# The output bias of an attention block, added by VectorE ahead of the product or by a matmul behind it

## What is computed

```python
A = jnp.sum(_cos_sim(K) * V, axis=-2)
Y = A[:, None, :] * Q
Y = Y @ W_out + b_out
return Y + X              # X is the row-normalised input here
# around it:
x = x + _layernorm(attn(_layernorm(x, axis=-1), ...), axis=-1)
x = x + _layernorm(ffn(_layernorm(x, axis=-1), ...), axis=-1)
```

## Time and profile before

| | |
|---|---|
| time, median of 3 runs (lowest, highest) | 973.98 us (970.87, 974.26) |
| the profiled execution's own time | 972.4 us |
| its span, first to last instruction | 970.6 us |
| PE busy, matmuls | 890.0 us (92%), 4558 |
| DVE busy | 639.8 us (66%) |
| ACT busy | 435.9 us (45%) |
| POOL busy | 387.7 us (40%) |
| mean granted TensorE clock | 0.974 of full speed |

### The profile page before, as it was taken

One profiled execution on the slowest core, in us unless ns is written; L12 is line 12 of the kernel. 1 busy time (PEld: TensorE's weight loads), 2 busy tenths in 40 slices (PEclk: granted clock), 3 DMA queues, 4 the chain that ended last, 5 costly groups with the idle time before them and its releaser, 6 DMA issues.

```text
span 970.6 us, 14785 instructions
## 1 busy us (share of the span) xinstructions
PE 890.0 (92%) x4558; PEld 730.6 (75%) x4558; DVE 639.8 (66%) x1374; ACT 435.9 (45%) x829; POOL 387.7 (40%) x316
## 2 busy tenths in 40 slices
PE   1999999999999899899999888799999999998885
PEld 1788877877888577677777677688888888886663
DVE  5757967966965766457556567466665666563778
ACT  4145245245253232241222436366666666664454
POOL 3357356456454000000000000467777776751262
PEclk9999999999999899899999898799999999999998
DMA  8226878778644886876443889397788787869998
GB/s 294 87 88 238 306 261 300 282 272 313 214 155 174 334 345 225 309 260 230 161 141 119 316 326 270 91 236 143 147 149 160 147 148 138 153 98 313 369 165 225
DMA packets 88666, 211.12 MB, mean 218 GB/s; under 512 B 11512, under 2 KB 19960, under 8 KB 83472
## 3 DMA queue, kind: packets, MB, share of 16 engines
q1 hardware_dynamic: 64544, 164.45, 46.8%
q0 software_dynamic: 18208, 41.50, 23.6%
q10 hardware_dynamic: 5840, 4.23, 1.6%
HBM read 119.14 MB, written 91.01 MB: 217 GB/s over the span
## 4 chain that ended last, share of the span: by engine, by line
PE 46%; DVE 11%; issue 6%; ACT 6%; POOL 3%; DMA 3%; DVEq 0%; POOLq 0%; ACTq 0%
PE bank L1545 5%; PE bank L1546 4%; PE bank L1547 4%; PE bank L1745 4%; PE bank L1743 3%; PE bank L1744 3%; PE bank L1730 3%; PE bank L1762 3%; PE bank L1760 3%; PE bank L1761 3%; PE bank L1752 2%; PE bank L1540 2%; ACT n L732 2%; DMA c_lo<-shared_scratch 1%; DMA f_scratch<-fo 1%
## 5 line engine op out<-in xcount | busy, mean ns | idle before, releaser
L1494 POOL DMA_INDIRECT f_scratch<-ro,dst x71 | 112.5, 1584 | 53.0 <-issue 22.0
L1545 PE MATMUL bank<-wkv_hi,h_hi 128*128 128x512 f32 x256 | 101.2, 395 | 3.8 <-issue 3.8
L1546 PE MATMUL bank<-wkv_lo,h_hi 128*128 128x512 f32 x256 | 100.3, 392 | 0.0
L1547 PE MATMUL bank<-wkv_hi,h_lo 128*128 128x512 f32 x256 | 100.2, 391 | 0.0
L1486 POOL DMA_INDIRECT xr<-n_scratch,ids x71 | 70.0, 986 | 75.4 <-issue 49.6
L1287 DVE TENSOR_TENSOR ro<-bank,b2b 128x512 f32<-128x512 f32 x71 | 49.1, 692 | 64.8 <-PE bank L1762 54.2
L1743 PE MATMUL bank<-we,x_hi 128*128 x284 | 86.1, 303 | 0.1
L1745 PE MATMUL bank<-we,x_lo 128*128 x284 | 80.6, 284 | 0.0
L1744 PE MATMUL bank<-we,x_hi 128*128 x284 | 80.4, 283 | 0.0
L629 ACT ACTIVATE sq<-kb 128x512 f32<-128x512 f32 x32 | 20.2, 633 | 125.9 <-DVE kb L930 125.9
L1545 PE MATMUL bank<-wo_hi,q_hi 128*128 128x512 f32 x128 | 54.7, 427 | 7.8 <-DVE fo L1119 4.2
(11 more groups left out here) (228 smaller groups left out, 2534.4 us busy)
## 6 DMA issues: line engine op xcount, KB each, us to landing
xg<-in_X SPq DMA_DIRECT2D x16, 1024.0 KB, 7.9
we<-expert_scratch SPq DMA_DIRECT2D x6, 2048.0 KB, 12.2
w_lo<-in_w SPq DMA_DIRECT2D x16, 512.0 KB, 5.5
expert_scratch<-w_hi SPq DMA_DIRECT2D x16, 512.0 KB, 2.8
expert_scratch<-w_lo SPq DMA_DIRECT2D x16, 512.0 KB, 4.1
q_scratch<-qh SPq DMA_DIRECT2D x8, 1024.0 KB, 3.9
q_scratch<-qb SPq DMA_DIRECT2D x8, 1024.0 KB, 6.0
q_hi<-q_scratch SPq DMA_DIRECT2D x8, 1024.0 KB, 4.8
```

The lines of the kernel that those rows point to most:

```text
L1494: pool.indirect_dma_start(f_dram, bass.IndirectOffsetOnAxis(dst[:, i:i + 1], 0), ro[i % NRO][:, :], None, compute_op=ALU.add).then_inc(r_s ...
L1545: pe.matmul(dst, hi(k), w_hi(k), start=(k == 0), stop=False)
L1546: pe.matmul(dst, hi(k), w_lo(k), start=False, stop=False)
L1547: last = pe.matmul(dst, lo(k), w_hi(k), start=False, stop=(k == KD - 1 and not more))
```

## The change

The matmul per tile goes (32 in all), and `bo` becomes a tile of 128 rows that all hold the bias in float32, loaded by one broadcast DMA. DVE's one operation per tile becomes two. `z_start` multiplies the input by its reciprocal deviation and adds the bias, all from SBUF, and `z_tile` adds the bank to that once the product is there. In a step z_start of tiles 0 and 1 stands ahead of z_tile 0, that of tile 2 ahead of z_tile 1, and that of tile 3 ahead of z_tile 2. The two operations each of ACT and DVE that prepared `bo` go.

```diff
-        bo = at("bo", 108, [B_ROWS, D], F32R)
+        bo = at("bo", 108, [P, D])
...
-            sp.dma_start(bo_raw[:, :], b_out.partition_broadcast(B_ROWS)).then_inc(late_in, 16)
+            sp.dma_start(bo[:, :], b_out.partition_broadcast(P)).then_inc(late_in, 16)
...
-            act.wait_ge(late_in, 96)
-            act.activation(bo_hi[:, :], bo_raw[:, :], ACT.Copy).then_inc(bo_hi_done, 1)
-            act.wait_ge(consts_set, BO_ZERO)
-            act.activation(bo[0:1, :], bo_raw[0:1, :], ACT.Copy).then_inc(bo_split, 1)
...
+            def z_start(g, j):
+                if j == 0:
+                    if g >= 2:
+                        dve.wait_ge(x2_stored[g % 2], 16 * (g // 2))
+                        dve.wait_ge(n3_ready, GT * (g - 1))
+                    dve.wait_ge(x_in[g % 2], 16 * (NG // 2 + g // 2 + 1))
+                    if g == 0:
+                        dve.wait_ge(late_in, 96)
+                dve.scalar_tensor_tensor(z[g % 2][:, j, :], xg[g % 2][:, j, :], rs[:, g, 1, j:j + 1], bo[:, :],
+                                         ALU.mult, ALU.add).then_inc(z_started, 1)
+
             def z_tile(g, j):
                 n = o_use["y", g, j]
-                if j == 0 and g >= 2:
-                    dve.wait_ge(x2_stored[g % 2], 16 * (g // 2))
-                    dve.wait_ge(n3_ready, GT * (g - 1))
+                dve.wait_ge(z_started, GT * g + j + 1)
                 dve.wait_ge(o_full, n + 1)
...
-                dve.scalar_tensor_tensor(z[g % 2][:, j, :], xg[g % 2][:, j, :], rs[:, g, 1, j:j + 1], o_[n % 3][:, :],
-                                         ALU.mult, ALU.add).then_inc(o_free, 1)
+                dve.tensor_tensor(z[g % 2][:, j, :], o_[n % 3][:, :], z[g % 2][:, j, :], ALU.add).then_inc(o_free, 1)
...
+                z_start(s, 0)
+                z_start(s, 1)
                 z_tile(s, 0)
+                z_start(s, 2)
                 z_tile(s, 1)
                 if s >= 1:
                     n_lo_parts(s - 1, (0, 1))
+                z_start(s, 3)
                 z_tile(s, 2)
...
-                        lambda k: wo_hi[b][:, k, :], lambda k: wo_lo[b][:, k, :], more=True)
-                if s == 0 and j == 0:
-                    pe.wait_ge(bo_split, 2)
-                pe.matmul(o_[n % 3][:, :], ones_f[0:B_ROWS, :], bo[:, :], start=False, stop=True).then_inc(o_full, 1)
+                        lambda k: wo_hi[b][:, k, :], lambda k: wo_lo[b][:, k, :]).then_inc(o_full, 1)
```

More of the change, by code:

```diff
@@ L166, in sandwich_kernel @@
         q_hi = [at(f"q_hi{i}", kb_, [P, KD, G], F32R) for i, kb_ in enumerate((56, 64))]
-        B_LO, B_ROWS = 32, 64
-        bo_raw, bo_hi = at("bo_raw", 140, [B_ROWS, D]), at("bo_hi", 142, [B_ROWS, D], F32R)
-        bo = at("bo", 108, [B_ROWS, D], F32R)
+        bo = at("bo", 108, [P, D])
         lgt = at("lgt", 104, [P, G])
@@ L309, in sandwich_kernel @@
         consts_set, iotas_set = sem("consts_set"), sem("iotas_set")
-        HALF_SET, ONES_SET, PICK_SET, BO_ZERO, GATE_ZERO, F_ZERO, ZEROS_SET = range(1, 8)
+        HALF_SET, ONES_SET, PICK_SET, GATE_ZERO, F_ZERO, ZEROS_SET = range(1, 7)
         x_in = [sem(f"x_in{i}") for i in range(2)]
@@ L331, in sandwich_kernel @@
         q_hi_done, q_split = sem("q_hi_done"), sem("q_split")
-        bo_hi_done, bo_split = sem("bo_hi_done"), sem("bo_split")
         o_full, o_free = sem("o_full"), sem("o_free")
         zv_ready, zr_ready = sem("zv_ready"), sem("zr_ready")
-        x2_ready, xv_ready, xr_ready, xnm_ready, n3_ready = (
-            sem("x2_ready"), sem("xv_ready"), sem("xr_ready"), sem("xnm_ready"), sem("n3_ready"))
+        z_started, x2_ready, xv_ready, xr_ready, xnm_ready, n3_ready = (
+            sem("z_started"), sem("x2_ready"), sem("xv_ready"), sem("xr_ready"), sem("xnm_ready"), sem("n3_ready"))
         x2_stored, n3_stored, f_stored = [sem(f"x2_stored{i}") for i in range(2)], sem("n3_stored"), [sem(f"f_stored{i}") for i in range(4)]
@@ L997, in _ @@
                         lo_part(n)
[L998 to L1002, removed]
                 k_tile(g, 1)
@@ L1033, in _ @@
                .then_inc(gw_split, 1)
+            def z_start(g, j):
[8 more added lines that the diff above has]
+                                         ALU.mult, ALU.add).then_inc(z_started, 1)
             def z_tile(g, j):
                 n = o_use["y", g, j]
-                if j == 0 and g >= 2:
-                    dve.wait_ge(x2_stored[g % 2], 16 * (g // 2))
-                    dve.wait_ge(n3_ready, GT * (g - 1))
+                dve.wait_ge(z_started, GT * g + j + 1)
                 dve.wait_ge(o_full, n + 1)
-                if j == 0:
-                    dve.wait_ge(x_in[g % 2], 16 * (NG // 2 + g // 2 + 1))
-                dve.scalar_tensor_tensor(z[g % 2][:, j, :], xg[g % 2][:, j, :], rs[:, g, 1, j:j + 1], o_[n % 3][:, :],
-                                         ALU.mult, ALU.add).then_inc(o_free, 1)
+                dve.tensor_tensor(z[g % 2][:, j, :], o_[n % 3][:, :], z[g % 2][:, j, :], ALU.add).then_inc(o_free, 1)
                 dve.wait_ge(o_free, 3 + n + 1)
```

## The result

The changed kernel takes 976.02 us (median of 20 runs, 972.36 to 980.64) against 973.30 (20 runs, 970.87 to 975.25): ratio 1.0028, interval 1.0016 to 1.0041. Run again beside others (e11) it gave 1.0027 (1.0011 to 1.0044). By the medians it is 2.7 us slower, and 1 lies outside both intervals. The forecast was 976.9. Its profiled execution took 973.87 us with a span of 972.1, which is 1.5 us above the profiled execution before (972.4 and 970.6). Its executions differ among themselves: of the twelve in e11 seven took 971.9 to 973.9 us at a mean granted clock of 0.966 to 0.969, and five took 976.0 to 979.1 us at 0.963 to 0.965.

The account below looks back on a forecast made before the run. TensorE was taken to set the pace, level with DVE at the start of even steps. A gain of 2.85 us and 5.7 us of fallen clock gave +2.9 on the 973.98 median: 976.9 us, range 970.0 to 981.0.

Parts of the forecast that it names:

- Which engine is level with which: At the start of even steps TensorE and DVE are level; DVE's path grows 1.88 us, TensorE idles 3.5 us.
- The bias costs 0.61 or 0.50 us, not 0.23: The bias matmul on TensorE costs 0.61 us, 0.50 where transposes follow, against 0.23 for a plain matmul.
- Step 0 and the first halves of steps 1 and 3 give nothing: Removed matmuls there gain 0 us, since the transposes behind them wait for n, which hangs on DVE work.
- The sum without the clock: -2.85: Over the loop, odd steps gain 6.66 us and steps 2, 4 and 6 lose 3.81: 2.85 us gained.
- The fallen clock: +5.7: Behind waits of 3.5 us in steps 2, 4 and 6 TensorE's clock falls, costing 1.9 us each, 5.7 together.
- the fourth fall: Rival, chance 0.17: thin activity drops the clock again behind a 1.6 us wait in step 1; 980.3 us.
- Rival (a), the clock holds: Chance 0.25: the clock holds at some or all of the three even-step waits; 971.1 to 974.9 us.
- Rival (b), 13.3 us gained if the additions hide: Chance 0.08: DVE catches up ahead of n_lo, so TensorE gains the other tiles too; 960.7 us.
- Rival (d): Chance 0.05: the 0.61 us is a bank-change cost, a removed matmul is worth 0.23; sum +7.9, 981.9 us.

Follow-up runs that it names:

- e11: The changed kernel run again beside others, against the kernel before: ratio 1.0027 (1.0011 to 1.0044).
- e3: Kernel before, bias matmul kept, plus one SBUF operation per tile on DVE in the places of z_start: 980.79 us, ratio 1.0094.
- e5: Changed kernel with the four z_start of steps 2, 4 and 6 moved ahead of the previous step's last filling piece: 958.62 us, ratio 0.9907.
- e1: Kernel before with the bias matmul reading 128 rows (126 of them zero) in place of 64: 965.83 us, ratio 0.9932.
- e2: Kernel before without the bias matmul and nothing in its place, so the output lacks that bias: 961.69 us, ratio 0.9893.
- e8: Changed kernel, z_start of steps 2, 4, 6 moved earlier, n_lo ahead of z_tile 1 there, two step 0 z_start earlier: 955.96 us, ratio 0.9874.
- e4: Changed kernel with 13 unread matmuls filling TensorE's wait ahead of the second transposes in steps 2, 4 and 6: 968.14 us, ratio 0.9946.
- e6: Changed kernel, z_start of steps 2, 4, 6 moved into DVE's idle time and n_lo ahead of z_tile 1 there: 959.25 us, ratio 0.9906.
- e9: Repeat of the changed kernel with the four z_start of steps 2, 4 and 6 in DVE's idle time: 962.79 us, ratio 0.9912.
- e10: Repeat of the changed kernel with z_start in idle time and n_lo ahead of z_tile 1 in steps 2, 4, 6: 962.36 us, ratio 0.9888.

## Why the prediction was right, and where its terms were off

The forecast was 2.9 us slower, and 2.7 was measured. Its steps against the runs:

- **Which engine is level with which.** Right. In the even steps DVE's row to n_lo grew by 1.87 us (1.88 forecast), and TensorE's wait is 3.40 (3.5 forecast). e3 lengthens the wait to 2.21 us by the DVE half alone, e5 brings it to 1.4 by moving the same work.
- **The bias costs 0.61 or 0.50 us, not 0.23.** Right in size and in cause (e1). Ahead of transposes it is a little more than 0.50, since the transposes behind a full product take 1.03 us instead of 1.09.
- **Step 0 and the first halves of steps 1 and 3 give nothing.** Right for the changed kernel: DVE's last z of step 0 starts at 327.00 (326.83 forecast) and TensorE waits for n in step 1, and in step 3 the transposes come 5.70 us after its first matmul where it was 5.71. It is z_start that makes it so. e1 and e2 gain there, and two z_start taken out of that row (e8) bring step 1's transposes forward.
- **The sum without the clock: -2.85.** Mis-sized. e4, in which the clock holds at these three waits, has a loop 4.12 us shorter than before; the table below says where. Tile 3 is worth 0.76 at the end of step 7, not 0.61. The same 0.15 is missing in the three stretches to n_lo, each of which is 1.12 us longer and not 1.27. Tile 2 of the odd steps gives 0.25 more in all than four times 0.50, and step 1's first and step 3's first transposes each come some 0.2 us sooner than forecast.
- **The fallen clock: +5.7.** 5.15 by e4 against the first profile: 1.1, 2.4 and 1.6 us in steps 2, 4 and 6, where 1.9 was taken for each. In e11 the fourth fall adds 1.6.
- **Together.** Both terms were too high, by 1.3 and by 0.55 us, and the loop of the first profile is 1.0 us longer where the sum said 2.9; that of the second, with its fourth fall, is 2.6 longer. The mechanism is right, but that the medians' 2.7 us lie so near 2.9 is in part luck: they hold executions like e11's, with a fall that the sum left out, and time outside the loop. Single profiles cannot divide it.
- **Rival (a), the clock holds.** Refuted for 3.4 us: it fell behind all six waits of that length in two profiles. The Trainium skill (TensorE: Matmul & The Clock Gate, Loop structure matters more than you think) says that the copy does no harm in a loop whose next matmuls follow immediately, and here they did not: TensorE waited for DVE. Behind such waits of up to 1.57 us in steps 2, 4 and 6 the clock held, behind 3.4 it did not.
- **Rival (b), 13.3 us gained if the additions hide.** Not what the change did, but e8 gains as much in the loop, 14.0 us, by place alone.
- **Rival (d)**, that the removed matmul is worth only 0.23 us, is refuted by e1.

The loop in eight stretches, each from the second transposes of one step to those of the next; the first begins at step 1's first matmul, and the last ends at the first transposes behind step 7. All in us, read from the traces; "forecast" is the prediction's sum without the clock.

| stretch, up to | forecast | e4 minus before | changed minus e4 | e11 minus e4 |
|---|---|---|---|---|
| step 1 | -0.50 | -0.74 | +0.08 | +1.70 |
| step 2 | +1.27 | +1.13 | -0.02 | -0.02 |
| step 3 | -1.11 | -1.32 | +1.13 | +2.48 |
| step 4 | +1.27 | +1.12 | 0.00 | +0.01 |
| step 5 | -2.22 | -2.33 | +2.39 | +1.35 |
| step 6 | +1.27 | +1.12 | 0.00 | -0.01 |
| step 7 | -2.22 | -2.34 | +1.57 | +1.18 |
| end | -0.61 | -0.76 | 0.00 | 0.00 |
| sum | -2.85 | -4.12 | +5.15 | +6.69 |

The two columns on the right are the price of the clock: differences stand only in stretches that begin behind a long wait or, in e11's step 1, hold one, and there a fall costs 1.1 to 2.5 us. Step 3's stretch also holds a wait for a DMA, whose end moves by some tenths of a us from trace to trace.

## What to carry to other kernels

Cost an instruction by where it stands on its engine: with the same 32 operations the change made the kernel 0.3% slower when twelve of them stood behind the wait of a late engine, and 0.9% faster when these twelve stood ahead of it. When work moves from the busiest engine to another, look for the places where the two already hand over to each other without slack, for there the gain and the loss add up to one wait. Such a wait can also lower TensorE's clock: behind waits of 2.2 to 3.4 us that cost another 1.1 to 2.5 us here, except for one of 2.21 us behind which the clock held. Read a matmul's price from start to start with its neighbours: here the odd shape of one operand cost more than the matmul, and widening it with zeros got back 0.7% at no cost elsewhere.

## What the runs showed of the hardware

- A matmul whose operand has 64 rows between operands of 128 takes 0.61 us from start to start with its neighbours where one of 128 rows takes 0.23 to 0.24 (e1).
- TensorE's clock held behind the waits of 1.17 to 1.57 us in steps 2, 4 and 6, fell to the 1.2 GHz level behind two of three waits of 2.21, behind all five of 2.37 to 2.57 in step 1 (e5, e6, e9, e10, e11, each with another low stretch some 4 us ahead of the wait), and behind all six of 3.40 to 3.44. Filling 3.4 us of wait with 13 matmuls that nobody reads kept it at 2.4 GHz and made the kernel 0.8% faster than the changed one.
- How long the clock stays down differs between executions of one kernel, and that can decide whether a later wait is long enough for another fall (2.57 us and a fall, 1.28 and none, in the same place of the same kernel). In one execution too: behind the changed kernel's three waits of 3.4 us it cost 1.1, 2.4 and 1.6 us.
- The length of a wait does not decide it alone. In e2 eight transposes take 1.16 us behind a wait of 1.57 in step 6, where matmuls ran without a gap ahead of it. Behind step 7 three waits follow each other with only four transposes between two of them, and the eight behind the third, of the same 1.57 us, take 1.97. The four behind the second wait are slow already (1.12 us where the first four took 0.66):

```profile
489.24 1.16 PE L1540 MATMUL bank<-ident,n 128*128 128x128 f32 x8 [1.57 <-DVE n_lo L1085]
...
534.92 0.66 PE L1540 MATMUL bank<-ident,n 128*128 128x128 f32 x4 [1.55 <-ACT n L732]
536.99 1.12 PE L1540 MATMUL bank<-ident,n 128*128 128x128 f32 x4 [1.41 <-DVE lg L1091]
539.68 1.97 PE L1540 MATMUL bank<-ident,n 128*128 128x128 f32 x8 [1.57 <-DVE n_lo L1085]
```
